# Input split moved up a unit, query tiles of every second column, and the first two probability tiles of a half added in one step, in a 16-image attention kernel

## The reference, cut to what matters

```python
# x: (16, 512, 32, 32) float32; 8 heads of 64; S = 32 * 32 = 1024 positions
xr = x.reshape(B, C, S).transpose(0, 2, 1)
qkv = (xr @ w_qkv + b_qkv).reshape(B, S, N_HEADS, 3 * d_k)
q, k, v = jnp.split(qkv, 3, axis=-1)
attn = jnp.einsum('bihd,bjhd->bijh', q, k) * d_k ** (-0.5)
attn = jax.nn.softmax(attn, axis=2)
out = jnp.einsum('bijh,bjhd->bihd', attn, v).reshape(B, S, N_HEADS * d_k)
out = (out @ w_proj + b_proj).transpose(0, 2, 1).reshape(B, C, H, W)
return out + x
```

## Time and profile before

| | |
|---|---|
| median of three runs | 3989.09 us |
| profiled execution, its own time | 3987.98 us |
| its span, first instruction to last | 3985.9 us |
| PE busy | 99% of the span |
| DVE, POOL, ACT busy | 83%, 75%, 74% |
| granted PE clock | 0.997 |

### The profile page before, as it was taken

The page is one execution under the profiler, slowest core; times in us unless marked ns, Lnnn a source line. Parts: engine busy times, 40 slices in busy tenths (PEclk is TensorE's granted clock), DMA queues, the critical chain, the costliest instruction groups (busy, mean ns, idle before and its releaser), DMA issues.

```text
span 3985.9 us, 60063 instructions
## 1 busy us (share of the span) xinstructions
PE 3936.3 (99%) x18464; PEld 3360.4 (84%) x18464; DVE 3319.5 (83%) x4449; ACT 2935.8 (74%) x5529; POOL 3006.5 (75%) x2371
## 2 busy tenths in 40 slices
PE   8999999999999999999999999999999999999998
PEld 6878888888888888888888888888888888888886
DVE  7788888888888888888888888888888888888887
ACT  5777777777777777777777777777777777777775
POOL 4678777777777777777777777877778777787775
PEclk9999999999999999999999999999999999999999
DMA  6344444434443344443444444444344434444432
GB/s 201 85 108 112 125 107 110 118 95 132 110 120 104 99 131 112 111 113 96 132 105 127 107 107 111 116 128 107 95 121 112 129 100 108 112 110 127 113 93 79
DMA packets 262943, 451.23 MB, mean 113 GB/s; under 512 B 107872, under 2 KB 118112, under 8 KB 258656
## 3 DMA queue, kind: packets, MB, share of 16 engines
q1 hardware_dynamic: 262624, 447.39, 42.4%
HBM read 204.48 MB, written 41.42 MB: 62 GB/s over the span
## 4 chain that ended last, share of the span: by engine, by line
PE 89%; issue 4%; DVE 4%; ACT 2%; DMA 1%; POOL 0%; SPq 0%; ACTq 0%; DVEq 0%
PE ps_g L473 24%; PE s L495 11%; PE ps_o L517 11%; PE ps_o L515 11%; PE st L574 11%; PE st L572 10%; PE ps_g L489 9%; DVE acc L806 2%; PE st L501 1%; PE st L502 1%; ACT p_hl L731 1%; ACT x_h L690 1%; ACT p L728 0%; DVE acc L803 0%; DVE qk_l L787 0%
## 5 line engine op out<-in xcount | busy, mean ns | idle before, releaser
L963 POOL TENSOR_TENSOR p_hl<-p,p_hl 128x512 fp32r<-128x512 f32 x2048 | 2609.0, 1298 | 915.0 <-ACT p_hl L731 914.4
L728 ACT ACTIVATE p<-st 128x512 f32<-128x512 f32 x2048 | 1231.8, 601 | 705.3 <-PE st L574 678.5
L809 DVE TENSOR_REDUCE nm<-s 128x1 fp32r<-128x1024 f32 x1024 | 1250.1, 1221 | 381.6 <-PE s L495 370.8
L806 DVE TENSOR_TENSOR acc<-acc,p 128x512 f32<-128x512 f32 x1792 | 1234.1, 689 | 25.5 <-DVE acc L803 0.5
L731 ACT ACTIVATE p_hl<-st 128x512 fp32r<-128x512 f32 x2048 | 1237.7, 604 | 0.0
L515 PE MATMUL ps_o<-p_hl,v_hl 128*128 128x512 f32 x2048 | 802.9, 392 | 4.5 <-POOL p_hl L963 3.9
L574 PE MATMUL st<-q,k 128*128 128x512 f32 x2048 | 804.4, 393 | 0.0
L517 PE MATMUL ps_o<-p_hl,v_hl 128*128 128x512 f32 x2048 | 802.0, 392 | 0.0
L572 PE MATMUL st<-q,k 128*128 128x512 f32 x2048 | 799.6, 390 | 1.4 <-DVE v_hl L794 1.1
L473 PE MATMUL ps_g<-x_h,wq 128*128 128x512 f32 x2016 | 711.5, 393 | 6.4 <-DVE qk_l L787 6.3
L495 PE MATMUL s<-k,q 128*128 128x512 f32 x2048 | 646.7, 396 | 9.0 <-DMA k<-qk_l 4.7
(11 more groups left out here) (192 smaller groups left out, 3756.8 us busy)
## 6 DMA issues: line engine op xcount, KB each, us to landing
k<-qk_h SPq DMA_DIRECT2D x256, 256.0 KB, 4.3
wq<-wq_d SPq DMA_DIRECT2D x126, 512.0 KB, 4.5
ring<-x_in SPq DMA_DIRECT2D x128, 256.0 KB, 3.7
q<-qk_h SPq DMA_DIRECT2D x128, 256.0 KB, 3.8
q<-qk_l SPq DMA_DIRECT2D x128, 256.0 KB, 4.9
k<-qk_l SPq DMA_DIRECT2D x128, 256.0 KB, 5.1
q<-q SPq DMA_DIRECT2D x256, 128.0 KB, 4.9
rinv<-rinv_d SPq DMA_DIRECT2D x256, 128.0 KB, 2.9
```

What stands on the lines that cost most here:

```text
L728: nc.scalar.activation(p[:, to, :], st[slot % RING][:], ACT.Exp)
L806: nc.vector.tensor_tensor(acc[:], acc[:], probs, ALU.add).then_inc(acc_done, 1)
L809: nc.vector.tensor_reduce(nm[:, it:it + 1], s1[:], AXX, ALU.max, negate=True).then_inc(max_done, 1)
L963: nc.gpsimd.tensor_tensor(p_l[:, to, :], p[:, to, :], p_h[:, to, :].bitcast(f32), ALU.subtract).then_inc(pl_done, 1)
```

## The change

It has four parts.

1. `first_scores` takes a query tile from every second column of 256 neighbouring queries: eight bytes from one to the next, not sixteen. `store_max` follows: each partition now writes two pairs of numbers to places 1 KB apart, so it has twice as many pieces of half the size.
2. `add_probs` no longer copies the first tile of a half. Where the copy stood, DVE does nothing; at the place of the second tile one instruction adds tiles 0 and 1 from `p` into `acc`, and counts for two.
3. `X_SPLIT` becomes 44: chunk 0, 45: 1, 46: 2 and 3, 47: 4, 48: 5, 49: 6, 50: 7. ACT splits ahead of the exponentials of the unit (behind `move_half`, where there is one). DVE splits as the last thing in the unit, behind the reading out of the group. POOL splits where it did.
4. `X_LOAD` brings chunks 4 to 7 in units 45 to 48, not 46 to 49.

```diff
-    X_SPLIT = {44 + c: c for c in range(CHUNKS)}
-    X_LOAD = {c + (40 if c < XRING else 42): c for c in range(CHUNKS)}
+    X_SPLIT = {44: (0,), 45: (1,), 46: (2, 3), 47: (4,), 48: (5,), 49: (6,), 50: (7,)}
+    X_LOAD = {c + (40 if c < XRING else 41): c for c in range(CHUNKS)}
...
-                sp.dma_start(max_d[n].rearrange("(p t) -> p t", p=P), nm[:, 4 * n:4 * n + 4].bitcast(f32)
+                sp.dma_start(max_d[n].rearrange("(a p t) -> p a t", a=2, p=P),
+                             nm[:, 4 * n:4 * n + 4].bitcast(f32).rearrange("p (a t) -> p a t", a=2)
...
-                    mm = nc.tensor.matmul(s1[:, cols(n)], q1[head % 2][:, it // 4 * HALF + it % 4:(it // 4 + 1) * HALF:4],
+                    mm = nc.tensor.matmul(s1[:, cols(n)], q1[head % 2][:, it // 2 * 2 * P + it % 2:(it // 2 + 1) * 2 * P:2],
...
+                    for c in X_SPLIT.get(U, ()) if B.ahead else ():
+                        i = c % XRING
+                        act.wait_ge(x_loaded[i], at(16 * CHUNKS // XRING, 16 * (c // XRING + 1)))
+                        act.wait_ge(qk_done, at(16, 15 + c // KT))
+                        split_x(c, ring[i][:])
                     for e in range(2):
                         slot, to = B.slot(U, e), U % 2 * 2 + e
...
-                probs = p[:, unit % 2 * 2 + e, :]
+                probs = [p[:, unit % 2 * 2 + i, :] for i in range(2)]
+                if unit % 4 == 0 and e == 0:
+                    return
                 dve.wait_ge(st_free, B.at(SLOTS, B.slot(unit, e) + 1))
-                if unit % 4 == 0 and e == 0:
+                if unit % 4 == 0:
...
-                    nc.vector.tensor_copy(acc[:], probs).then_inc(acc_done, 1)
+                    nc.vector.tensor_tensor(acc[:], probs[0], probs[1], ALU.add).then_inc(acc_done, 2)
```

More of the change, by code:

```diff
@@ L758, in body @@
                         take_row(half, st[slot % RING])
[L759 to L764, removed]
                     if U in OS_SPLIT and B.before:
@@ L797, in add_probs @@
             def add_probs(B, unit, e):
-                probs = p[:, unit % 2 * 2 + e, :]
+                probs = [p[:, unit % 2 * 2 + i, :] for i in range(2)]
+                if unit % 4 == 0 and e == 0:
+                    return
                 dve.wait_ge(st_free, B.at(SLOTS, B.slot(unit, e) + 1))
-                if unit % 4 == 0 and e == 0:
+                if unit % 4 == 0:
                     if (v := B.at(HALVES, unit // 4)) is not None:
                         dve.wait_ge(accl_done, v)
-                    nc.vector.tensor_copy(acc[:], probs).then_inc(acc_done, 1)
+                    nc.vector.tensor_tensor(acc[:], probs[0], probs[1], ALU.add).then_inc(acc_done, 2)
                 else:
                     dve.wait_ge(acc_done, B.at(2 * UNITS, 2 * unit + e))
-                    nc.vector.tensor_tensor(acc[:], acc[:], probs, ALU.add).then_inc(acc_done, 1)
+                    nc.vector.tensor_tensor(acc[:], acc[:], probs[e], ALU.add).then_inc(acc_done, 1)
             def maximum(it):
@@ L887, in body @@
                         invert(half % 2, at(16 * HEADS, 16 * (half // 2 + 1)))
[L888 to L893, removed]
                     if U in WP_SPLIT and B.first:
@@ L917, in body @@
                         low_last(*OS_LAST[U], list(OS_LAST).index(U) + 1)
+                    for c in (c for c in X_SPLIT.get(U, ()) if B.ahead and c not in X_POOL):
+                        k, n = c % KT, c // KT
+                        dve.wait_ge(x_high, at(CHUNKS, CHUNKS + c + 1))
+                        nc.vector.tensor_tensor(xs[1][:, k, cols(n)], ring[c % XRING][:], xs[0][:, k, cols(n)].bitcast(f32),
+                                                ALU.subtract).then_inc(x_low[1], 1)
             bodies(body)
@@ L966, in body @@
                         normalise(B, pair, U % 16 // 4)
-                    if U in X_SPLIT and B.ahead and X_SPLIT[U] in X_POOL:
-                        c = X_SPLIT[U]
+                    for c in (c for c in X_SPLIT.get(U, ()) if B.ahead and c in X_POOL):
                         pool.wait_ge(x_high, at(CHUNKS, CHUNKS + c + 1))
```

## The result

The changed kernel takes 3996.14 us, the median of 20 runs (3974.68 to 4004.32), against 3988.27 for 20 runs of the kernel before. The ratio is 1.0017, with a 95% interval of 1.0009 to 1.0025: 8 us slower, at the edge of what can be told from no change. I had forecast 3954, and 3930 to 3972 as the range. The profiled execution took 3974.68 us, the shortest of the 20; a second execution was traced later, and it took 3996.23.

The account below looks back on a forecast made before the run. PE, busy 99% of the span, was taken to set the time. Gains of 29 us (tiles) and 6 us (splits), with add and store at 0, took 3987.98 to 3953, by the median 3954; range 3930 to 3972.

Parts of the forecast that it names:

- the new add's term: DVE's add replacing copy and old add: waits for one POOL instruction, ends about as before; nothing gained on the path.
- POOL gets in twice: Rival: POOL's second remainder goes ahead of the new add; PE stalls 0.6 us in each of 256 halves, 4105; chance 0.04.
- My own test for the add: Sign for the new add: well over 0.689 us on average, near 1.2, with L787 of unit 37 where it was.
- The tiles: Query tile weights in first scores at 8 bytes, not 16: 35 ns less a plain unit, 29 us gained in all.
- as the rival has it: Rival on query tile weight loads: any gather costs 309 ns, so the 29 us stay; 3982, chance 0.10.
- is hidden already: Query tile weight loads: one losing a fifth of its excess over 188 ns costs no step time, so all 35 ns counted.
- The slow steps behind L495: PE steps after L495, laid to its late weight load; rival that they stay gives back 16 us, 3970, chance 0.10.
- The store at no cost: `store_max` with twice the pieces: landing of 1.4 us might double, against some 11 us of slack; cost 0.
- The splits: Moved input splits, units 44 to 52: waits fall from 1.79 to 1.4 us an image; gain 6 us.

Follow-up runs that it names:

- the plain tile: Changed kernel with the first-tile copy and old add restored, query tiles of 128 neighbouring queries, maxima stored in 4-byte pieces; 5416.96 us, ratio 1.359.
- the copy back: Changed kernel with the first-tile copy and the old add restored, query tiles and splits still changed; 3962.18 us, ratio 0.994.
- the remainder moved: Changed kernel, new adds kept, POOL's output-projection input remainders in units 0, 1, 2 and 4 instead of 1 to 4; 3967.07 us, ratio 0.9953.

## Why the prediction was wrong

**The step that failed** is the new add's term, put at nothing on the path because the add gets its turn after one instruction of POOL. What happened is close to the rival "POOL gets in twice", but I gave that 0.04 and priced it at 0.6 us in each of 256 halves. It comes in one half of 16, at 2.15 us or 3.75, some 33 us in a run near the median. Its argument was that DVE got its turn after one instruction of POOL "wherever a row shows it"; that is evidence on the places read, and I had worked the new add out at unit 37 alone, where POOL has a pair of instructions and then idles. The trace of before showed the place that is different. POOL's timeline of the kernel before, image 5, units 4 to 6, then the old add on DVE in the midst of it:

```profile
1289.88 2.57 POOL L963 TENSOR_TENSOR p_hl<-p,p_hl 128x512 fp32r<-128x512 f32 x2
1292.39 1.30 POOL L974 TENSOR_TENSOR os_hl<-o,os_hl 128x512 fp32r<-128x512 f32 x1
1293.65 5.05 POOL L963 TENSOR_TENSOR p_hl<-p,p_hl 128x512 fp32r<-128x512 f32 x4
```

```profile
1293.98 0.68 DVE L806 TENSOR_TENSOR acc<-acc,p 128x512 f32<-128x512 f32 x1
```

Seven instructions without a gap, 1289.88 to 1298.70. The old add, with one input in a bank, took its usual 0.68 us among them; the new one can wait until POOL has nothing left. Had the rival been priced there, at 2.15 us in 15 images, it would have been 32 us, nearly all of the 35 us of gain in my sum, at a chance that nothing in the trace could fix.

A run of POOL without a gap isn't enough to lose the turn. In unit 21 of the changed kernel POOL has an L975 and a pair of remainders behind it just as in unit 5. Image 5, DVE, then POOL:

```profile
1355.96 0.70 DVE L806 TENSOR_TENSOR acc<-p 128x512 f32<-128x512 f32 x1
```

```profile
1354.82 1.29 POOL L975 TENSOR_TENSOR os_hl<-o,os_hl 128x512 fp32r<-128x512 f32 x1
1356.07 3.00 POOL L965 TENSOR_TENSOR p_hl<-p,p_hl 128x512 fp32r<-128x512 f32 x2
```

There the add asks 0.15 us before POOL's instruction ends, and it went ahead of the pair in every image after the first, in both traces of the changed kernel (0.72 us at most).

My own test for the add would have passed it. I asked for a mean near 1.2 us; the rows are 1139 ns in the profiled execution and 1241 in the second:

```profile
L806 DVE TENSOR_TENSOR acc<-p 128x512 f32<-128x512 f32 x256 | 291.5, 1139 | 4.0
```

```profile
L806 DVE TENSOR_TENSOR acc<-p 128x512 f32<-128x512 f32 x256 | 317.6, 1241 | 3.9
```

A mean over 256 hides 14 of 3.5 us. The rest of that step held: with the splits moved nothing was gained on the path, and the adds at unit 37 took 1.26 us where I worked out 1.23.

**The tiles** were right in mechanism and mis-sized: 20 ns a plain unit for 35, in 15 images 14 us alone and some 17 beside the splits, not 29. (Without that gain my sum is 3982, as the rival has it; the 3981 in the prediction is a slip.) The choice that a load a little over the plain 188 ns "is hidden already" was wrong, as the plain tile shows. The slow steps behind L495 did go with the late load; what stayed is at L496 itself.

**The store at no cost** failed in a place that I hadn't looked at. Its landing went from 1.4 us to 3.2, more than double:

```profile
max_d<-nm SPq DMA_DIRECT2D x256, 2.0 KB, 3.2
```

In the steady images this is hidden, as said. In image 0 it isn't. SP's timeline there in the changed kernel, and PE's unit 12; then SP's in the kernel before:

```profile
82.99 0.37 SPq L279 DMA_DIRECT2D max_d<-nm  x1
...
89.89 0.24 SPq L284 DMA_DIRECT2D q<-max_d  x1
```

```profile
93.17 0.77 PE L573 MATMUL st<-q,k 128*128 128x512 f32 x1 [2.79 <-issue]
```

```profile
82.39 0.33 SPq L279 DMA_DIRECT2D max_d<-nm  x1
...
87.53 0.24 SPq L283 DMA_DIRECT2D q<-max_d  x1
```

Weights still stream in there, the load of the maxima is issued 6.9 us behind their store and not 5.1, and PE stands 2.79 us at the scores that use the maxima. With the tile of every second column it stood 2.1 to 3.0 us at this place in all nine traces; before it stood 0.26, with the new add alone 0.25, and with the splits alone 0.15. The profile names no releaser, so that the store is the cause rests on this comparison.

**The splits** came out as worked, and a little better. I had L474 of unit 48 released 2.47 us behind the unit's start; it was 1457.35 - 1455.03 = 2.32, still by the output group. The two splits took 3.21 us for my 3.3, and the wait of unit 50 vanished. In sum 0.67 us an image for my 0.4.

Without the add, then, the sum would have been 3954 + 12 for the tiles + 3 for the store - 4 for the splits = 3965; the copy back measured 3962. The remaining 34 us are the add.

## What to carry to other kernels

An operation that newly has to wait its turn behind another engine's instructions must be priced where that engine runs longest without a gap, and its price can be the time until that engine has nothing left that doesn't itself wait for the operation, not one instruction; go through every place where it falls, in the trace of before. Watch the longest of such instructions, not their mean, and suspect a turn that is won in one execution and lost in the next when one kernel's executions spread by 30 us. A transfer that is hidden in the steady part must be looked at again at the start, where the weights still stream in.

## What the runs showed of the hardware

A waiting DVE instruction isn't served in order of asking. With POOL's instructions back to back it was passed over for all that stood there (3.5 us), or served after the one that ran (0.99 us), and which differs between executions of one program. With the remainder moved it ran at once (0.68 us) in 14 images although the record of a POOL instruction had opened 0.34 us before. The Trainium skill, page "SBUF — State Buffer", section "Who interferes with whom", says that a DVE instruction with two SBUF inputs contends with a GpSimd instruction that reads SBUF, and that issue order decides who blocks. The traces agree that the one kept out waits for the end of an instruction of the other: an add ended 0.56 us behind POOL's. They don't bear out issue order, as far as the records' starts show it: by that the add, asked for at 1292.07, would have gone ahead of POOL's instruction of 1292.49, and it didn't; and with the remainder moved it would have gone behind the POOL instruction that was there first, and it didn't.

A store of 2 KB landed in 1.4 us in pieces of 16 bytes and in 3.2 us in pieces of 8; with pieces of 4 the load behind it came 8.4 us after it.

Weights at 4 bytes from column to column, the plain case, load in 188 ns, at 8 bytes in 194, at 16 in 309; yet those at 8 bytes still cost 0.02 us a unit over those at 4. The Trainium skill's rule that fp32 may be strided by 4 for free, which stands in the section "Door 1: The DMA port swizzle" of the same page, is not borne out by these numbers.

PE's clock was granted at 0.50 for some 3 us behind a stall of about 2 us in some images (1 and 5 of the profiled execution) and not in others (12 and 14), with the same work ahead of it.
